# One fp32 product of probabilities and values, 31 expert blocks, the down product in the same turn, and the last sums on three engines

## The reference, cut to what matters

```python
scores = jnp.einsum('bsghd,btgd->bghst', q, k) * scale
p = jax.nn.softmax(scores, axis=-1)
return jnp.einsum('bghst,btgd->bsghd', p, v)      # probabilities times values
...
# each of the two attentions goes through this; the result is divided by proj_smooth,
# rounded to the fp8 grid and multiplied by wproj
...
# experts: the two best of 16 by the router's logits, softmax over the two,
# silu(z Wg) * (z Wu), times Wd, summed with the two weights into the residual
```

## Time and profile before

| | us |
|---|---|
| median of 3 runs | 554.91 (548.64 to 555.04) |
| the profiled execution's own time | 553.87 |
| its span (first to last instruction) | 552.1 |
| PE busy | 435.9 (79% of the span) |
| DVE busy | 405.2 (73%) |
| ACT busy | 309.9 (56%) |
| POOL busy | 293.5 (53%) |

### The profile page before, as it was taken

How to read it: one execution, slowest core, us unless ns; L and a number is a source line. 1 busy time by engine, 2 the same in 40 slices (tenths; PEclk the granted TensorE clock), 3 DMA queues, 4 the chain that set the end, 5 groups by cost and what they waited for, 6 DMA issues and landing times.

```text
span 552.1 us, 10895 instructions
## 1 busy us (share of the span) xinstructions
PE 435.9 (79%) x3238; PEld 314.1 (57%) x3238; DVE 405.2 (73%) x1071; ACT 309.9 (56%) x642; POOL 293.5 (53%) x546
## 2 busy tenths in 40 slices
PE   0457875989898988998898989888878779999940
PEld 0323553656565655665565656565668658787830
DVE  4757756688989889889898888989976655222245
ACT  2456775567776676776775677668783031333320
POOL 1028354385576575676568566666562046046670
PEclk9977887899999999999999999999987678999985
DMA  8900029999900000000000000000048012334407
GB/s 212 313 27 2 0 35 193 305 293 292 267 4 0 0 0 0 0 0 0 0 0 0 0 0 0 0 2 1 2 170 345 2 57 95 98 92 128 123 25 228
DMA packets 34812, 45.68 MB, mean 83 GB/s; under 512 B 3034, under 2 KB 32223, under 8 KB 33888
## 3 DMA queue, kind: packets, MB, share of 16 engines
q1 hardware_dynamic: 26656, 35.61, 21.1%
q0 software_dynamic: 6992, 9.46, 7.8%
q10 hardware_dynamic: 1136, 0.27, 0.3%
HBM read 28.34 MB, written 24.32 MB: 95 GB/s over the span
## 4 chain that ended last, share of the span: by engine, by line
PE 57%; DVE 15%; ACT 11%; issue 7%; DMA 7%; POOL 1%; ACTq 1%; SPq 0%; POOLq 0%; DVEq 0%
PE proj_ps L852 12%; PE score_ps L875 8%; PE proj_ps L1004 8%; PE out_ps L911 6%; PE proj_ps L844 6%; PE headT_ps L866 4%; ACT qT L681 4%; DMA wp_sb<-in_wpT 3%; ACT vf L652 3%; DMA rowv<-in_rowc 2%; PE pv_ps L900 2%; DVE ys L1197 2%; DVE yv L1251 2%; PE pv_ps L902 1%; PE pv_ps L901 1%
## 5 line engine op out<-in xcount | busy, mean ns | idle before, releaser
L852 PE MATMUL proj_ps<-arena 128*128 128x512 f16 x384 | 103.3, 397 | 5.2 <-DMA wp_sb<-in_wpT 4.6
L1220 DVE BATCH_NORM_STATS2 st<-rot 128x6 f32<-128x128 f32 x384 | 83.0, 279 | 30.8 <-ACT rot L644 29.3
L866 PE MATMUL headT_ps<-idf,rot 128*128 128x128 f32 x384 | 60.2, 280 | 32.8 <-ACT qT L681 30.6
L644 ACT ACTIVATE rot<-proj_ps 128x512 f32<-128x512 f32 x96 | 57.0, 594 | 50.5 <-PE proj_ps L852 46.5
L866 PEld LDWEIGHTS headT_ps<-idf,rot 128*128 128x128 f32 x384 | 44.5, 142 | 56.5 <-issue 39.1
L520 POOL TENSOR_TENSOR rot<-rot,cw 128x512 f32<-128x512 f32 x64 | 70.5, 1122 | 2.5
L875 PEld LDWEIGHTS score_ps<-kT,qT 128*128 128x128 f32 x512 | 65.3, 203 | 8.1 <-ACT qT L681 5.1
L531 POOL TENSOR_TENSOR reg<-reg,rinv 128x512 f32<-128x512 f32 x32 | 33.4, 1042 | 63.8 <-DVE rinv L1244 63.8
L875 PE MATMUL score_ps<-kT,qT 128*128 128x64 f32 x512 | 65.2, 284 | 0.0
L852 PEld LDWEIGHTS proj_ps<-arena 128*128 (+1 forms) x384 | 38.8, 106 | 35.2 <-issue 12.3
L681 ACT ACTIVATE qT<-headT_ps,colv 128x512 f32<-128x512 f32 x64 | 49.3, 770 | 12.2 <-PE headT_ps L866 12.2
(11 more groups left out here) (226 smaller groups left out, 929.6 us busy)
## 6 DMA issues: line engine op xcount, KB each, us to landing
zbuf<-fill SPq DMA_DIRECT2D x1, 16576.5 KB, 61.1
arena<-in_wffn SPq DMA_DIRECT2D x4, 1536.0 KB, 12.4
arena<-zbuf SPq DMA_DIRECT2D x32, 128.5 KB, 2.1
wkv_stage<-in_wkvN SPq DMA_DIRECT2D x1, 2048.0 KB, 15.1
wp_sb<-in_wpT POOLq DMA_DIRECT2D x1, 2048.0 KB, 15.6
wp_sb<-ybuf SPq DMA_DIRECT2D x8, 256.0 KB, 4.5
xs<-in_x SPq DMA_DIRECT2D x2, 512.0 KB, 5.1
wp_sb<-in_wqN POOLq DMA_DIRECT2D x1, 1024.0 KB, 12.9
```

The costliest lines, as they stand in the source:

```text
L644: act.activation(raw[c % 2][i], proj_ps[i % 2][:, :], ACT.Copy).then_inc(proj_evac, 1)
L852: mm = pe.matmul(ps, lhs, w[kind][:, ch, 512 * b:512 * b + 512], start=(k == 0), stop=(k == 3))
L866: mm = pe.transpose(dst, raw[c % 2][i][:, h * D:(h + 1) * D], idf[:, :])
L1220: ins = ve.bn_stats(st[:, 4 * i + h, :], raw[c % 2][i][:, h * D:(h + 1) * D])
```

## The change

The values are kept as one fp32 tensor `vv` and the transposed probabilities as fp32 too. So ACT's fp16 copy of the values, POOL's rest (`values_low`) and DVE's rest (`prob_low`) are gone, PE makes one fp32 product in place of three fp16 ones, and it now waits for ACT's copy of the probabilities (`prob_out`) and for the values (`v_full`).

The number of blocks goes from 32 to 31: the last unit has one block, and its steps are cut to half their width. The down product of unit u now stands in turn u, behind the transposes of unit u+2's rows; in ACT's queue the copy of the transposed hidden rows of u-1 goes ahead of the silu of u; on DVE the copy of the down product follows one unit behind, no longer two. In the last sums DVE adds the first expert row, ACT scales the second by its weight, and POOL adds it.

```diff
-NBLK = 32
+NBLK = 31
+NPAIR = (NBLK + 1) // 2
...
+def blocks(s):
+
+    return range(min(2, NBLK - 2 * s))
...
-        vf = sb("vf", [P, 2, 512], F32)
-        vh = sb("vh", [P, NU, 512], F16)
-        vl16 = sb("vl16", [P, NU, 512], F16)
+        vv = sb("vv", [P, NU, 512], F32)
...
-            def values_low(t, c):
-                n = NU * t + c
-                gp.wait_ge(v_hi, n + 1)
-                gp.tensor_tensor(vl16[:, c, :], vf[:, c % 2, :], vh[:, c, :], ALU.subtract).then_inc(v_lo, 1)
...
+            for t in range(NT):
+                gp.wait_ge(second_done, t + 1)
+                gp.wait_ge(first_done, t + 1)
+                xt = xs[:, t * H:(t + 1) * H]
+                gp.tensor_tensor(xt, xt, yg[:, t, 1, :], ALU.add).then_inc(y_ready, 1)
...
-            def values_high(t, c):
+            def values_out(t, c):
 
                 n = NU * t + c
                 act.wait_ge(proj_done, 4 * n + 4)
-                ge(act, v_lo, n - 1)
+                ge(act, pv_done, n - 3)
                 scale = col("s_v") if c < 2 else 1.0 / WKV_SCALE
-                act.activation(vf[:, c % 2, :], proj_ps[1][:, :], ACT.Copy, scale=scale).then_inc(v_full, 1)
-                act.wait_ge(v_full, n + 1)
-                ge(act, pv_done, n - 3)
-                act.activation(vh[:, c, :], vf[:, c % 2, :], ACT.Copy).then_inc(v_hi, 1)
+                act.activation(vv[:, c, :], proj_ps[1][:, :], ACT.Copy, scale=scale).then_inc(v_full, 1)
...
-            def prob_high(w, s):
+            def prob_copy(w, s):
                 act.wait_ge(probT_done, w + 1)
                 ge(act, pv_done, w - 1)
-                act.activation(probT[s][:, 0:512], probT_ps[:, :], ACT.Copy).then_inc(prob_hi, 1)
+                act.activation(probT[s], probT_ps[:, :], ACT.Copy).then_inc(prob_out, 1)
...
             for u in range(NSHU, NUNIT):
-                unit_silu(u)
                 if u > NSHU:
                     unit_hidT(u - 1)
-                if u - NSHU + 2 < NBLK // 2:
+                unit_silu(u)
+                if u - NSHU + 2 < NPAIR:
                     block_rows(u - NSHU + 2)
...
+            act.wait_ge(coef_ready, 2)
+            for t in range(NT):
+                act.wait_ge(yg_ld[t], 16)
+                act.activation(yg[:, t, 1, :], yg[:, t, 1, :], ACT.Copy, scale=coef[:, t, 1:2]).then_inc(second_done, 1)
...
-                pe.wait_ge(prob_lo, w + 1)
-                pe.wait_ge(v_lo, w + 1)
+                pe.wait_ge(prob_out, w + 1)
+                pe.wait_ge(v_full, w + 1)
...
-                        o = pv_ps[b][:, g * P:(g + 1) * P]
-                        lo = 512 + g * P
-                        vhi, vlo = vh[rows, u, g * D:(g + 1) * D], vl16[rows, u, g * D:(g + 1) * D]
-                        pe.matmul(o, vhi, pT[rows, g * P:(g + 1) * P], start=True, stop=False)
-                        pe.matmul(o, vhi, pT[rows, lo:lo + P], start=False, stop=False)
-                        mm = pe.matmul(o, vlo, pT[rows, g * P:(g + 1) * P], start=False, stop=True)
+                        mm = pe.matmul(pv_ps[b][:, g * P:(g + 1) * P], vv[rows, u, g * D:(g + 1) * D],
+                                       pT[rows, g * P:(g + 1) * P], start=True, stop=True)
...
-                if u - NSHU + 2 < NBLK // 2:
+                if u - NSHU + 2 < NPAIR:
                     block_transposes(u - NSHU + 2)
-                if u > NSHU:
-                    unit_down(u - 1, bases[u - 1])
-            unit_down(NUNIT - 1, bases[NUNIT - 1])
+                unit_down(u, bases[u])
...
-            def prob_low(w, s):
-                ve.wait_ge(prob_hi, w + 1)
-                ve.tensor_tensor(probT[s][:, 512:1024], probT_ps[:, :], probT[s][:, 0:512],
-                                 ALU.subtract).then_inc(prob_lo, 1)
...
-                if live(n, 3):
-                    prob_low(n - 3, (c - 3) % 2)
...
-            for u in range(4, NUNIT):
+            for u in range(4, NSHU):
                 unit_hidden(u)
                 unit_out(u - 2)
-            unit_out(NUNIT - 2)
+            unit_out(NSHU - 2)
+            unit_out(NSHU - 1)
+            for u in range(NSHU, NUNIT):
+                unit_hidden(u)
+                if u > NSHU:
+                    unit_out(u - 1)
...
                 ve.wait_ge(yg_ld[t], 16)
-                for k in range(TOPK):
-                    ins = ve.scalar_tensor_tensor(xt, yg[:, t, k, :], coef[:, t, k:k + 1], xt, ALU.mult, ALU.add)
-                    if k == 0:
-                        link(ins)
-                ins.then_inc(y_ready, 1)
+                ve.scalar_tensor_tensor(xt, yg[:, t, 0, :], coef[:, t, 0:1], xt, ALU.mult, ALU.add).then_inc(first_done, 1)
```

More of the change, by code:

```diff
@@ L55 @@
 NSHU = NT
-NUNIT = NSHU + NBLK // 2
+NUNIT = NSHU + NPAIR
 COL = {}
@@ L1046, in block_transposes @@
                     pe.wait_ge(z_evac, 6)
-                for b in range(2):
+                for b in blocks(s):
                     for c in range(HC):
```

68 lines of the change are left out of this document (37 added, 31 removed).

## The result

| | before | after |
|---|---|---|
| median of the runs compared | 552.48 (548.64 to 555.04, 4 runs) | 566.42 (565.58 to 568.12, 4 runs) |
| profiled execution (its span) | 553.87 (552.1) | 566.58 (564.8) |
| start of the first block's up product | 476.11 | 459.86 |
| from there to the last unit's up product | 50.03 | 79.71 |
| to the landing of the last scatter | 13.24 | 9.23 |

The ratio on record is 1.0286, 95% interval [1.0229, 1.0344]: slower, where 560 us (about no change) was forecast. The two medians of the table, 13.9 us apart, give 1.0252, which lies in the interval too. Between the two profiled executions the difference is 12.7 us, and the table splits it: -16.3, +29.7, -4.0, +0.8 and +2.4.

A forecast was written before the change was run, and what follows sets the result against it. PE alone was taken to bound the expert blocks, PE and DVE in turn the attention rounds. Terms -16.8 + 23 - 0.2 = +6 on 553.87 gave 560 us; range 547 to 575, the main forecast's own 553 to 567.

The forecast's parts named there:

- value products, a step: Attention steps: 16 fp32 instructions of 0.107 us, array halves side by side, 0.86 against 0.78 us; +0.19 taken, bound +1.04.
- DVE's rest, the long step: Attention round's long step: removing DVE's fp16 rest of the probabilities, ahead of the softmax, saves 0.61 us.
- start of the first block: Attention rounds and router ahead of the expert blocks: shorter rounds and last value product's wait, together -16.8 us.
- wait for ACT, a turn: Expert blocks: down product waits for ACT's hidden rows' copy, queued behind the rows' copy; +1.2 us a turn.
- table loads, a turn: Expert blocks: PE's loads come after the down product's wait, only partly covered; +0.8 us a turn, bounds 0 and 1.0.
- last sums: Kernel's end: 24 operations split evenly over DVE, ACT and POOL; -0.2 us, bounds -0.5 and +0.6.
- Rival 2: Expert blocks: PE's idle pieces make the clock fall; if in a third of turns, +15, 575 us; chance 0.1.
- Rivals 1, 3 and 4: Alternative outcomes: Serial halves 582 us, chance 0.12; Free table loads 549, chance 0.15; rival 4 536, chance 0.06.
- Serial halves: Value products: fp32 halves run one after another, 0.85 us more a step, some +22, 582 us; chance 0.12.
- Free table loads: Expert blocks: loads cost nothing, only the down product's wait remains; 11 us less, 549 us; chance 0.15.
- rival 4: Expert blocks: both the down product's wait and the table loads hide; 536 us; chance 0.06.
- the 0.47 for which ACT idled: Attention's long step: ACT's idling for the values' projection, which PE did late after waiting 1.66 us, goes; -0.47 us.

The follow-up runs named there:

- with four tiles: The changed kernel with POOL adding only for tiles 0 to 3 and DVE alone summing tiles 4 to 7: 564.56 us, ratio 1.0196.
- the hidden rows first: The changed kernel with ACT copying the transposed hidden rows of unit u ahead of the rows of unit u+2: 551.98 us, ratio 0.9983.
- The stand-in: Unused DVE subtraction replacing the probabilities' rest, both operands in SBUF, added to the kernel with only the fp32 values changed: 557.89 us, ratio 1.0041.

## Why the forecast was wrong, step by step

| term | forecast | measured |
|---|---|---|
| value products, a step | +0.19 | +0.31 (1.09 against 0.78) |
| ACT's copy, an ordinary step | -0.53 | -0.47 to -0.65 |
| DVE's rest, the long step | -0.61 | -0.60 |
| a round | 42.5 | 42.86 |
| start of the first block | -16.8 | -16.3 |
| wait for ACT, a turn | +1.2 | +1.21 |
| table loads, a turn | +0.8 | +0.75 |
| last up product, after the first | +27 | +29.7, of it 3.6 by the clock |
| behind it, to the last landing | -4 | -4.0 |
| last sums | -0.2 | +0.8, then +2.4 at the end |

Of the 6.7 us between the forecast's sum (559.9) and the 566.6 of the profiled execution, 3.5 are in the last sums and the end, 2.7 in the blocks and 0.5 in the start of the blocks.

**The first step that failed is the last sums**: "For the last tile two DVE operations of 0.46 in a row become one, ACT beside it, then 0.6 on POOL: -0.2, bounds -0.5 and +0.6". It priced the chain to the last output and left out what stands behind it. POOL now works last, so its closing instruction, to which the sum gave nothing, sets the end: +2.4, outside the bounds. POOL's own add was 0.72, above the 0.6 taken. The +0.8 in the chain can't be put down to the divided sums: with the old sums in the same kernel it was 12.96 against 13.13, and over the nine kernels with the old sums that stage varied from 12.3 (before, the lowest) to 13.0 us.

**The second step that failed is the clock in the blocks, left out of the sum.** Rival 2 came in part. I gave the fall of the clock 0.10 as a case of its own, in a third of the turns, and the main sum took it at nothing. It happened in 2 of 14 turns and cost 3.6 us; without it the blocks would have come out at 26.1, below the 27 forecast. Among the kernels here that kept both idle pieces (1.05 and 0.57 us) the blocks had two, four, one and two falls; in those with one piece or none, none. A cost that comes in part belongs into the sum with a part of its price. With 3.6 for the clock and 2.4 for the end the forecast would have stood at 566.

**Rivals 1, 3 and 4.** Serial halves would have shown 1.7 us groups: they took 1.09. That is still more than the 0.86 forecast, which took 16 instructions side by side at 0.107; the 16 starts lie in 0.89 us, and the next group comes 0.2 behind the last. The forecast's remark that the scores' weight loads are about as long as their spacing of 0.11 is a misreading: the trace has them at 0.19 to 0.20 us. Free table loads would have given turns of 4.6: that time came only when the loads were moved away. Nothing hid the wait for ACT, so rival 4 is out.

**What was right, and how far by luck.** The start of the blocks came out within 0.6 us of the forecast. The six full rounds gained 13.0 us (forecast 12.6 and 0.8 for the clock), all the rest 3.3 (forecast 3.4). Inside a round two errors met: the long step with its follower gained 1.48 (forecast 1.4), the two other steps 0.33 together (forecast 0.68); and the fall of the clock in the one round went whole, 1.6 where I had counted 0.8. Of the three terms of the long step and its follower two have a run of their own: DVE's rest 0.60 (0.61 forecast) and ACT's copy 0.4 (0.53), which, put back, lengthened the follower by 0.65 and shortened the long step by 0.22. The third, the 0.47 for which ACT idled, no run shows alone. And since that start differs by up to 9 us between kernels with the same attention stage, a hit within 0.6 us is partly chance.

## What to carry to other kernels

Where an engine is busy 99% of a stage, reordering its queue so that a product needs a result of its own turn costs the whole latency of the other engine's copy, every turn; before such a move, read what stands ahead of that copy in the other queue and which register loads stand behind the new wait. Price an edit at the end of a kernel up to the end of the span, the closing instruction of the engine that now works last included. Where two idle pieces a turn appear in a stage that had none, put some falls of the clock into the sum itself.

## What the hardware showed that I had not expected

**POOL's closing instruction ends 4.3 to 4.4 us behind POOL's last work**, be that a scatter (538.3 to 542.7, before) or a sum (560.2 to 564.5 in the change, 556.8 to 561.2 with four tiles), in all 16 profiled kernels. In the changed kernel that of DVE takes 0.9 us and that of ACT 0.5. It cost nothing in the kernel where POOL's last sum ended 5.0 us before the last output landed.

**An idle piece can have the wrong name.** With the hidden rows first, the idle time ahead of the up product was put down to DVE, 0.52 to 0.79 us; when the table loads were moved as well, it vanished with nothing changed on DVE.

**A DVE operation with two SBUF operands can take twice its time beside POOL.** The stand-in took 0.68 to 0.72 us in 21 steps and 1.52 to 1.56 in 11. In all 11 POOL's multiplication (L526, also on SBUF operands) had started first, 0.03 to 0.51 us earlier, and DVE's operation ended 0.55 us behind POOL's. In 4 of the 21 POOL started 0.02 to 0.24 behind; then DVE was not slowed, and POOL's took 1.36 to 1.56 us, where its shortest and most frequent time is 1.03 to 1.04. The original operation, with one operand in PSUM, took 0.67 to 0.69 in all 32 steps. The Trainium skill ("SBUF — State Buffer", SBUF: two separate sides) says that DVE and GpSimd take a shared port pair for a whole instruction, whichever starts first, for a DVE operation with two SBUF inputs against a GpSimd one that reads SBUF. The trace agrees with it, in both directions of who starts first.

The same wait lies in the long step of every kernel here. DVE's last operation on the next inputs in the changed kernel:

```profile
249.97 1.28 DVE L1202 TENSOR_TENSOR arena<-ys,ym 128x1024 f16 x1 [0.16 <-DVE ys L1198]
```

Its namesake of the same line and size takes 0.69 us at 247.12. At 249.97 POOL's multiplication (L524) had begun 0.74 us earlier, and DVE's operation ends 0.55 behind it. It took 1.28 us in all six long steps of full rounds in each of the 16 profiled kernels, before the change too. DVE's time binds the long step, so about 0.6 us of each may be lost here; no run took POOL's operation away.
